# A planned instruction order: attention slots take only the time that stream stages leave

## The chip, the cores and the metric

The kernel runs on one NeuronCore of one Trainium2 chip. The metric is device time in microseconds (us) of one execution. The kernel before takes 3509.27 us, the median of three runs (3504.03 to 3510.40).

## The reference, cut to what matters

Four transformer layers in a row, in float32, on x of 4 batches x 1024 rows x 256 features. What bears on the change is the first layer (L0) and the last two (L2 and L3, which the kernel runs as one region):

```python
# L0: masked self-attention with 16 heads of 16, then cross-attention, then MLP
x = x + g_msa * (attn(q, k, v, mask) @ attn_out_W)
x = x + g_x * (attn(qc, kc, vc) @ co_W)              # 77 keys
x = x + g_mlp * (gelu(ln(x) @ mlp_W1 + mlp_b1) @ mlp_W2 + mlp_b2)
# L1: layernorm, 3 experts with a router, a gate; no attention over the rows
# L2: as L0 with full self-attention over 1024 keys, cross-attention, MLP
# L3: a further cross-attention over the 77 keys
x = x_q + (softmax(q k^T / 4) v) @ Wp + bp
```

In L0 the mask of this case leaves 256 of the 1024 keys alive, and the kernel finds that at run time and takes the short branch (`FEWR`). L2 works on all 1024 keys.

## The kernel before, in words

The work of a region (`FEWR` for L0; `L2R` for L2 and L3 together) is written as a list of tokens, `R.order`. All five engines walk the same list, each issuing its own part of every token, so the list is the program order on every engine. Each engine's queue is in order; a wait holds all that stands behind it.

There are two kinds of work:

- **Slots.** A slot is one step of self-attention for one key tile of 128 keys, 4 heads and 512 query rows: 4 score products (K=32 rows of the array each), ScalarE's 4 exponentials (line 1895), the 4 products with V of the slot before, and the "fills", score products `lead` slots ahead of which VectorE takes the row maximum (line 1564 in L2, 1561 in L0). L2 has 256 slots, 64 for each batch; L0 has 64, 16 for each batch. Some slots end with transposes: "nm" (line 1066) and "tail" (line 1055).
- **Stages of the streams.** Four streams prepare a batch (`p_tokens`: layernorm, V, Q and K). Eight streams (`o_tokens`: 4 batches x 2 halves of 512 rows) carry a half from its attention output to its end: output projection `oT`/`oP`, layernorm `lnA`/`lnB`/`lnT`, cross-attention, MLP `m1`/`m2`; in region L2 a second cross-attention (L3's) follows. Cross-attention is a chain: queries `cq`, maximum steps `cm` (4 per sequence, four VectorE reductions each, line 1717), `cn` (line 1180), exponentials `cs` (line 1943), products `cp`, transposes `ct` (line 1202). A stream of batch b opens when b's slots are over, so it runs beside the slots of batch b+1; the last batch's streams have no slots beside them. There are 12 cross-attention sequences beside slots in region L2 (3 batches x 2 halves x 2) and 6 in L0.

All matmuls of stages and slots take their PSUM bank from one ring of seven, in list order, and TensorE waits until the bank's last reader has freed it.

`overlapped(R)` (from line 525) is a planner that runs while the program is built. It keeps a clock `now`, gives every token a TensorE cost (`cost`: 3.2 us for a full slot of L2, 0.8 for `cm`, 6.9 for `m2`) and every dependence a latency (`needs`), and at each step places either the stage that has been ready longest or the next slot. A stage may be placed when it is ready and TensorE is free. What decides between a ready stage and a ready slot is a credit: each slot adds `R.share` (3.4 us in L2, 12.0 in L0, and never holds more), each stage takes its cost away, and with a credit of zero or less a ready slot goes first:

```python
state["credit"] = min(state["credit"] + R.share, R.share)     # place(), a slot
...
state["credit"] -= cost(R, tok)                                # place(), a stage
```

With a share of 3.4 the list of L2 has about one slot for every 3.4 us of stages as long as stages are ready. Going through the planner of the kernel before with its own costs, a slot is placed ahead of a ready stage 120 times among the 268 slot tokens of region L2, and 10 times among the 70 of L0. The order of layer 1 (`l1_order`) is written out by hand and has no planner.

Of the kernel before, what the change touches and what calls it, by code (L numbers as in the profile page):

```python
# [62 lines left out]
def pixart_kernel(nc, io):  # L63
    ctx = ExitStack()
    with ctx:
# [408 lines left out]
        def cost(R, tok):  # L474

            kind = tok[0]
            if kind == "slot":
                return (2.15 if tok[1] is not None else 0.0) + (1.05 if tok[2] is not None else 0.0) + 0.45 * len(tok[4]) + 0.45 * len(tok[5])
            if kind == "qk":
                return (3.4 if R.rope else 1.7) * (0.5 if tok[3] and R.few else 1.0)  # L480
            if kind == "v":
                return 1.7 if R.few else 3.5
            return {"lnT": 0.9, "oT": 0.9, "oP": 1.7, "cq": 1.7, "cm": 0.8, "cn": 0.5, "cs": 1.1, "cp": 1.1, "ct": 0.5, "m1": 3.4, "m2": 6.9}.get(kind, 0.0)
# [40 lines left out]
        def overlapped(R):  # L524
# [7 lines left out]
            state = {"now": 0.0, "t": -R.lead, "probs": 0, "turn": 0, "exp": 0.0, "credit": 0.0}  # L532
# [10 lines left out]
            def open_to(tok):  # L543

                t, kind = state["t"], tok[0]
                if kind in ("lnA", "lnB") and tok[1] == 0 and tok[2]:
                    b = tok[2]
                    if not all(k in ended for k in p_tokens(R, b - 1)):
                        return False
                if kind in ("lnB", "ct") and row_buffer(tok)[1]:  # L550
                    return rows[tok[-1]] is None
                if kind == "qk" and tok[1]:
                    return t >= (R.index(tok[1] - 1, 2 * tok[2] + 1, 1 if tok[3] else tok[4]) + 1) * R.per
                if kind == "v" and tok[1]:
                    if R.few:
                        return t > (tok[1] - 1) * R.total
                    return t > (R.index(tok[1] - 1, 2 * tok[2] + 1, 1) + 1) * R.per
                if kind == "oT" and tok[1] == 0:
                    return ("tail", R.index(tok[2], NG - 1, tok[3])) in ended and (tok[2] == 0 or all(k in ended for k in o_tokens(R, tok[2] - 1, tok[3])))
                if kind == "cs":  # L560
                    return state["probs"] == 0
                if kind == "cp":
                    return state["turn"] == 0
                return True

            def ready(tok):
                times = []
                for other, us in needs(R, tok):
                    if other not in ended:
                        return None  # L570
                    times.append(ended[other] + us)
                return max(times, default=0.0)

            def slot_ready():
                t, times = state["t"], [state["exp"]]
                fill = t + R.lead
                b, g, qh = R.block(fill // R.per)
                if fill < NB * R.total and fill % R.per == 0 and qh == 0 and g % 2 == 0:
                    for k in R.qk_steps(b, g // 2):
                        if k not in ended:  # L580
                            return None
                        times.append(ended[k] + (4.5 if R.rope else 2.0))
                if 1 <= t <= NB * R.total and (t - 1) % R.per == 0:
                    b, g, qh = R.block((t - 1) // R.per)
                    if ("v", b, 0 if R.few else g // 2) not in ended:
                        return None
                tok = slot_token(R, 0, NB * R.total, t)
                for q in tok[4]:
                    b, g, qh = R.block(q)
                    if b and ("oT", 0, b - 1, qh) not in ended:  # L590
                        return None
                return max(times)

            def place(tok):
                order.append(tok)
                kind = tok[0]
                state["now"] += cost(R, tok)
                ended[tok] = state["now"]
                if kind == "slot":
                    state["t"] += 1  # L600
                    state["credit"] = min(state["credit"] + R.share, R.share)
                    if tok[1] is not None:
                        state["exp"] = state["now"] + 1.1
                    for q in tok[4]:
                        ended["tail", q] = state["now"]
                elif kind in ("cs", "cp", "ct"):
                    state["probs"] += {"cs": 1, "cp": -1, "ct": 0}[kind]
                    state["turn"] += {"cs": 0, "cp": 1, "ct": -1}[kind]
                half, claim = row_buffer(tok)
                if half is not None:  # L610
                    rows[half] = tok if claim else None
                if kind != "slot" and state["t"] > 0:
                    state["credit"] -= cost(R, tok)
                for item in list(loads):
                    if item in loads and item[2] == 0.0 and all(k in ended for k in item[1]):
                        loads.remove(item)
                        place(item[0])

            def hidden_follows(tok):


                prior = next((k for k in reversed(order) if cost(R, k)), None)
                if tok[0] == "m1":
                    return tok[4] == 1 and prior == tok[:4] + (0,)
                return tok[0] == "cq" and R.l == 2 and tok[3] == 1 and prior == tok[:3] + (0,) + tok[4:]
# [5 lines left out]
            while state["t"] < end or any(h < len(s) for h, s in zip(heads, streams)):  # L631
                now = state["now"]
                for item in list(loads):
                    if item in loads and all(k in ended for k in item[1]) and max(ended[k] for k in item[1]) + item[2] <= now:
                        loads.remove(item)
                        place(item[0])
                found = []
                for n, s in enumerate(streams):
                    if heads[n] < len(s) and open_to(s[heads[n]]):
                        tok = s[heads[n]]  # L640
                        when = ready(tok)
                        if when is not None:
                            found.append((when, n, tok))
                free = [f for f in found if cost(R, f[2]) == 0.0 and f[0] <= now]
                if free:
                    when, n, tok = free[0]
                    heads[n] += 1
                    place(tok)
                    continue
                slot = slot_ready() if state["t"] < end else None  # L650
                work = sorted([f for f in found if f[0] <= now and cost(R, f[2])], key=lambda f: (not hidden_follows(f[2]), f[1] >= NB, f[0]))
                if work and (hidden_follows(work[0][2]) or slot is None or slot > now or state["credit"] > 0.0 or state["t"] <= 0):
                    when, n, tok = work[0]
                    heads[n] += 1
                    place(tok)
                elif slot is not None and (slot <= now or not work):
                    later = min([f[0] for f in found], default=slot)
                    if slot <= now or slot <= later:
                        state["now"] = max(now, slot)
                        place(slot_token(R, 0, NB * R.total, state["t"]))  # L660
                    else:
                        state["now"] = later
                else:
                    waits = [f[0] for f in found] + [max(ended[k] for k in item[1]) + item[2] for item in loads if all(k in ended for k in item[1])]
                    assert waits, (R.name, state, [s[h] for h, s in zip(heads, streams) if h < len(s)], loads)
                    state["now"] = min(waits) if min(waits) > now else now + 0.1
# [1486 lines left out]
```

## Time and profile before

| | us |
|---|---|
| median of three runs | 3509.27 |
| the profiled execution, its own time | 3505.52 |
| its span in the trace | 3503.7 |
| TensorE (PE) busy | 3300.4, 94% |
| VectorE (DVE) busy | 1840.0, 53% |
| ScalarE (ACT) busy | 1436.5, 41% |
| mean granted TensorE clock | 0.96 of full speed |

The span and what lies around it (1.8 us) make the profiled execution's own time. In the trace, preparation runs to about 100 us, region L0 to about 1000, layer 1 to about 1640, and region L2 from there to the end at 3503.7. The slots of region L2 lie between about 1700 and 3240 (its "nm" transposes, line 1066, run from 1700.4 to 3235); the streams of its first three batches start at about 1998. The rows on which the next section rests are below.

### The profile page before, as it was taken

The page shows a single profiled execution, that of the slowest core. Times are in us where ns is not written, and L with a number is a line of the kernel's source. Part 1 is how long each engine was busy: PE and PEld are TensorE (multiplying, and loading weights), DVE is VectorE, ACT ScalarE, POOL GpSimd, SP SyncE. Part 2 cuts the span into 40 slices and gives each one's busy share as a digit, 9 for nine tenths or more (in the row PEclk, how much of TensorE's full clock was granted, in tenths as well). Part 3 has the DMA queues.
Part 4 walks back from the last instruction along what each step waited for, and adds up shares of the span by engine and source line. Part 5 has one row for each costly group of instructions (what it writes and reads, how often), then busy time and mean ns, then how long its engine had stood idle before and what let it go on. Part 6 is the DMA issues. An engine that isn't in the chain of part 4 may idle for free.

```text
span 3503.7 us, 49090 instructions
## 1 busy us (share of the span) xinstructions
PE 3300.4 (94%) x19540; PEld 1823.4 (52%) x19540; DVE 1840.0 (53%) x3843; ACT 1436.5 (41%) x2607; POOL 244.6 (7%) x214
## 2 busy tenths in 40 slices
PE   6899999999889999998999999999999999999887
PEld 3555666657575666666433344534455344543364
DVE  4776544562412232324766775567755676556423
ACT  0344444344312222221355455554554645555333
POOL 1100100100100000001000010010100001010010
PEclk9999999989889999999899999999999999999898
DMA  5200000002000000001000000000000000000000
GB/s 166 90 6 1 8 20 4 25 1 95 16 22 1 0 1 0 1 1 55 1 1 1 1 7 4 1 25 7 7 4 16 10 7 7 4 16 16 1 1 13
DMA packets 57256, 57.99 MB, mean 17 GB/s; under 512 B 17728, under 2 KB 51248, under 8 KB 56764
## 3 DMA queue, kind: packets, MB, share of 16 engines
q1 hardware_dynamic: 57028, 54.79, 5.0%
q8 instruction: 163, 2.67, 0.3%
q14 instruction: 65, 0.53, 0.0%
HBM read 46.89 MB, written 7.89 MB: 16 GB/s over the span
## 4 chain that ended last, share of the span: by engine, by line
PE 89%; DVE 7%; ACT 2%; issue 1%; POOL 0%; DMA 0%; DVEq 0%; SPq 0%; ACTq 0%
PE ps L901 82%; PE ps L1075 3%; PE ps L1202 1%; DVE row_max_cross L1717 1%; PE ps L1055 1%; DVE max_halves L1564 1%; PE ps L1066 1%; ACT probs L1943 1%; DVE bn_stats L1618 1%; DVE xn_tok L1631 1%; DVE big L1723 1%; PE ps L1180 0%; ACT big L1895 0%; DVE bn_stats L1595 0%; DVE mean_var L1624 0%
## 5 line engine op out<-in xcount | busy, mean ns | idle before, releaser
L1895 ACT ACTIVATE big<-ps 128x512 f32<-128x512 f32 x1280 | 687.9, 598 | 795.1 <-PE ps L901 794.0
L901 PE MATMUL ps<-big 32*128 32x512 f32 (+2 forms) x5760 | 949.2, 603 | 15.9 <-DVE row_max L1561 4.3
L1564 DVE TENSOR_REDUCE max_halves<-ps 128x1 f32<-128x512 f32 x1024 | 653.0, 685 | 359.8 <-PE ps L901 359.0
L901 PEld LDWEIGHTS ps<-big 32*128 32x128 f32 (+1 forms) x5760 | 394.0, 188 | 497.5 <-issue 387.2
L901 PE MATMUL ps<-big,probs 128*32 128x512 f32 (+1 forms) x2688 | 378.7, 605 | 9.9 <-ACT big L1895 4.1
L901 PE MATMUL ps<-weights_mlp,big 128*128 128x256 f32 (+1 forms) x1248 | 334.7, 420 | 2.5 <-ACT big L1955 2.5
L901 PEld LDWEIGHTS ps<-weights_mlp,big 128*128 128x128 f32 x1248 | 235.4, 191 | 85.3 <-issue 57.0
L1601 DVE TENSOR_TENSOR x_tok<-ps,x_tok 128x512 f32<-128x512 f32 x112 | 77.4, 692 | 308.3 <-PE ps L901 308.3
L901 PE MATMUL ps<-x_T,weights_mlp 128*128 128x256 f32 x1024 | 229.6, 383 | 4.3 <-ACT x_T L1912 3.3
L1561 DVE TENSOR_REDUCE row_max<-ps 128x2 f32<-128x512 f32 x256 | 165.1, 686 | 128.0 <-PE ps L901 127.8
L1943 ACT ACTIVATE probs<-ps 77x512 f32<-77x512 f32 x384 | 196.4, 593 | 83.7 <-PE ps L901 83.7
L901 PEld LDWEIGHTS ps<-x_T,weights_mlp 128*128 128x128 f32 x1024 | 194.4, 191 | 37.4 <-issue 6.1
L901 PEld LDWEIGHTS ps<-big,probs 128*32 128x32 f32 (+1 forms) x2688 | 75.5, 113 | 236.7 <-issue 147.6
L2090 POOL TENSOR_SCALAR eps_tile<-mean_var 128x4 f32<-128x4 f32 x56 | 13.4, 240 | 2550.0 <-DVE mean_var L1624 2550.0
L1955 ACT ACTIVATE big<-ps,mlp_b 128x256 f32<-128x256 f32 x256 | 107.6, 471 | 180.4 <-PE ps L901 180.2
L1717 DVE TENSOR_REDUCE row_max_cross<-ps 128x4 f32<-128x308 f32 x384 | 155.1, 473 | 37.4 <-PE ps L901 36.6
L901 PE MATMUL ps<-big,k_v_cross 32*77 32x512 f32 (+1 forms) x832 | 155.8, 642 | 7.6 <-DVE big L1723 7.6
L901 PE MATMUL ps<-weights,x_T 128*128 128x256 f32 x640 | 159.2, 402 | 2.6 <-ACT x_T L1870 2.5
L901 PEld LDWEIGHTS ps<-weights,x_T 128*128 128x128 f32 x640 | 125.0, 201 | 43.9 <-issue 22.8
L901 PE MATMUL ps<-weights,big 128*128 128x256 f32 x640 | 145.5, 380 | 0.0
L1832 DVE SCALAR_TENSOR_TENSOR probs<-ps,o_T,probs 128x256 f32<-128x256 f32 x96 | 46.4, 484 | 178.2 <-PE ps L901 178.2
L2005 ACT ACTIVATE big<-ps,o_T 128x512 f32<-128x512 f32 x96 | 66.1, 688 | 177.5 <-PE ps L901 177.5
(223 smaller groups left out, 3387.9 us busy)
## 6 DMA issues: line engine op xcount, KB each, us to landing
weights_mlp<-in_L_xcond_mlp_W SPq DMA_DIRECT2D x5, 1024.0 KB, 5.3
weights_mlp<-in_L_xcond_W_mlp SPq DMA_DIRECT2D x5, 1024.0 KB, 5.4
x_tok<-in_x SPq DMA_DIRECT2D x4, 1024.0 KB, 9.4
out_y<-x_tok SPq DMA_DIRECT2D x8, 512.0 KB, 2.9
big<-in_L_xcond_e_w SPq DMA_DIRECT2D x3, 1024.0 KB, 9.8
gates_biases<-mod_rows SPq DMA_DIRECT2D x20, 128.0 KB, 5.2
big<-in_L_xcond_adaLN_W SPq DMA_DIRECT2D x1, 2304.0 KB
kc_groups<-x_tok SPq DMA_DIRECT2D x3, 616.0 KB, 7.4
```

The costliest lines, as they stand in the source:

```text
L901: return pe.matmul(out, lhsT, rhs, start=first, stop=last)
L1055: last = pe.transpose(PS[:, bank, i * P:(i + 1) * P], OT[:, c:c + P], ident[:, :])
L1075: last = pe.transpose(PS[:, banks[ft], (t % 4) * P:(t % 4 + 1) * P], rows[:, t, ft * P:(ft + 1) * P], ident[:, :])
L1561: dve.tensor_reduce(NM[:, 2 * qh + e, c:c + 2], PS[:, bank, :].rearrange("p (t n) -> p t n", t=2), AX.X, ALU.max, negate=True).then_inc(R. ...
L1564: dve.tensor_reduce(NMP[:, e, j, qt, hf:hf + 1], PS[:, bank, :], AX.X, ALU.max, negate=True).then_inc(R.frees(key), 1)
L1601: dve.tensor_tensor(x, PS[:, R.bank(key), :], x, ALU.add).then_inc(R.frees(key), 1)
L1717: dve.tensor_reduce(dst, src, AX.X, ALU.max, negate=True).then_inc(R.frees(key), 1)
L1832: dve.scalar_tensor_tensor(ROU[hf][:, t, :], PS[:, M.EXPERT[o % 2], 0:D], RP[:, 4 * hf + t, e:e + 1], ROU[hf][:, t, :], ALU.mult, ALU.add) ...
L1895: act.activation(PB[:, score % 2, j, :], PS[:, R.bank(key), :], ACT.Exp, scale=SCALE).then_inc(R.frees(key), 1)
L1943: act.activation(PC[0:NC, j, :], PS[0:NC, R.bank(key), :], ACT.Exp, scale=SCALE).then_inc(R.frees(key), 1)
L1955: last = act.activation(HT[hf][:, m, :], PS[:, R.bank(key), i % 2 * D:(i % 2 + 1) * D], ACT.Gelu_apprx_tanh, bias=B1[:, 0 if R.l == 0 else ...
L2005: act.activation(dst, PS[:, M.HIDDEN[q % 3], :], ACT.Silu, bias=ANC[:, m, b:b + 1]).then_inc(e_hsb, 1)
```

## The change

In `overlapped`, a ready stage no longer needs a credit. Whenever a stage is ready and TensorE is free in the plan, it is placed; a slot is placed when no stage is ready. The credit is still counted and has no effect. Costs, latencies, conditions for opening, and the engines' code for each token stay as they are, so every instruction is issued as often as before; only the order of tokens in regions L0 and L2 can differ. Layer 1 and the preparation don't change.

```diff
                 slot = slot_ready() if state["t"] < end else None
                 work = sorted([f for f in found if f[0] <= now and cost(R, f[2])], key=lambda f: (not hidden_follows(f[2]), f[1] >= NB, f[0]))
-                if work and (hidden_follows(work[0][2]) or slot is None or slot > now or state["credit"] > 0.0 or state["t"] <= 0):
+                if work and (hidden_follows(work[0][2]) or slot is None or slot > now or True):
                     when, n, tok = work[0]
```

## Rows read from the trace of the kernel before

**Rows 1.** The page: busy time of each engine, and its 40 slices.

```profile
PE 3300.4 (94%) x19540; PEld 1823.4 (52%) x19540; DVE 1840.0 (53%) x3843; ACT 1436.5 (41%) x2607; POOL 244.6 (7%) x214
...
PEclk9999999989889999999899999999999999999898
```

**Rows 2.** Stretches of region L2: us, engines' busy us, PEclk, DMA, GB/s.

```profile
1707.00:1990.00 283.00, 281.88 (x1764) 99.11 (x1764) 189.38 (x323) 148.57 (x280) 3.62 (x3) 1.00 0.00 1
1998.00:3240.00 1242.00, 1207.42 (x7948) 562.90 (x7944) 782.60 (x1532) 653.08 (x1192) 101.52 (x74) 0.99 0.03 9
3240.00:3504.00 264.00, 217.44 (x1228) 128.68 (x1227) 94.89 (x228) 92.56 (x172) 21.75 (x18) 0.86 0.01 5
```

**Rows 3.** Timeline of TensorE, slots alone: start us, us, what, count.

```profile
1745.07 2.93 PE L901 MATMUL ps<-big 32*128 32x512 f32 x16
1747.93 1.06 PE L901 MATMUL ps<-big,probs 128*32 128x512 f32 x8
1748.93 2.93 PE L901 MATMUL ps<-big 32*128 32x512 f32 x16
```

**Rows 4.** Groups by form, 1998 to 3240: busy, mean ns | idle before.

```profile
L1564 DVE TENSOR_REDUCE max_halves<-ps 128x1 f32<-128x512 f32 x716 | 459.7, 685 | 279.8 <-PE ps L901 279.0
L1895 ACT ACTIVATE big<-ps 128x512 f32<-128x512 f32 x723 | 390.9, 597 | 445.1 <-PE ps L901 444.7
...
L1717 DVE TENSOR_REDUCE row_max_cross<-ps 128x4 f32<-128x308 f32 x192 | 77.3, 474 | 10.7 <-PE ps L901 10.6
```

**Rows 5.** TensorE's waits, 1998 to 3240: total us, times, longest.

```profile
PE ps L901 <- ACT big L1895: 11.2, 16, 1.2
PE ps L901 <- DVE row_max_cross L1717: 9.0, 15, 0.7
```

**Rows 6.** Stretches with a fallen clock, and others, of 1998 to 3240.

```profile
1998.00:2028.00 30.00, 25.47 (x184) 14.06 (x180) 25.63 (x67) 9.54 (x18) 2.91 (x6) 0.83 0.06 14
...
2870.00:2900.00 30.00, 27.23 (x204) 13.32 (x200) 23.86 (x52) 12.09 (x23) 1.92 (x3) 0.94 0.07 19
2900.00:2950.00 50.00, 47.69 (x337) 18.39 (x334) 33.01 (x63) 27.59 (x52) 8.15 (x4) 0.93 0.00 1
...
3150.00:3180.00 30.00, 28.17 (x217) 13.69 (x210) 22.29 (x44) 13.99 (x27) 0.00 (x0) 0.94 0.00 1
```

**Rows 7.** Stretches of region L0, cross-attention and other stages in turn.

```profile
265.00:340.00 75.00, 69.75 (x649) 40.14 (x644) 52.49 (x103) 34.49 (x63) 0.00 (x0) 0.91 0.01 1
340.00:470.00 130.00, 129.18 (x776) 89.99 (x772) 65.32 (x149) 62.23 (x109) 12.25 (x13) 1.00 0.02 6
470.00:545.00 75.00, 68.76 (x556) 41.70 (x553) 44.50 (x90) 23.43 (x43) 7.78 (x5) 0.84 0.09 24
545.00:690.00 145.00, 144.53 (x889) 100.80 (x888) 70.19 (x143) 69.72 (x124) 9.74 (x9) 1.00 0.05 14
690.00:745.00 55.00, 48.76 (x429) 28.57 (x427) 32.45 (x71) 17.25 (x31) 7.65 (x5) 0.78 0.03 8
```

**Rows 8.** Exponentials of slots, 470 to 545, then 2080 to 2360.

```profile
L1895 ACT ACTIVATE big<-ps 128x512 f32<-128x512 f32 x16 | 8.7, 597 | 26.4 <-PE ps L901 26.4
...
L1895 ACT ACTIVATE big<-ps 128x512 f32<-128x512 f32 x157 | 84.9, 597 | 95.5 <-PE ps L901 95.4
```

**Rows 9.** Timeline of TensorE: three maximum steps in a row, then two.

```profile
2877.72 0.81 PE L901 MATMUL ps<-k_v_cross,x_T 32*128 32x154 f32 x16 [0.76 <-ACT big L1895]
2879.14 0.81 PE L901 MATMUL ps<-k_v_cross,x_T 32*128 32x154 f32 x16 [0.61 <-DVE row_max_cross L1717]
2880.68 1.41 PE L901 MATMUL ps<-k_v_cross,x_T 32*128 32x154 f32 x16 [0.74 <-DVE row_max_cross L1717]
...
2626.13 0.81 PE L901 MATMUL ps<-k_v_cross,x_T 32*128 32x154 f32 x16 [0.76 <-ACT big L1895]
2627.55 0.81 PE L901 MATMUL ps<-k_v_cross,x_T 32*128 32x154 f32 x16 [0.61 <-DVE row_max_cross L1717]
```

**Rows 10.** A stretch of region L0 at the fallen clock.

```profile
525.00:539.00 14.00, 13.19 (x119) 7.70 (x116) 7.61 (x19) 2.65 (x5) 0.00 (x0) 0.52 0.00 1
```

## The prediction

> **What bounds the kernel now.** I read the page first: TensorE is busy 94% of the span, VectorE 53%, ScalarE 41%, and the granted clock is nine tenths or more in all but a few slices [rows 1]. The chain of waits says the same; nearly all of it is TensorE's matmuls. A new order changes no instruction, so it can move the time only through what TensorE loses between and around its work: idle time, and time at the lower of its two clock levels (1.2 in place of 2.4 GHz). The second thing to read is therefore a table of stretches, and from it these two losses.
>
> In region L2 the slots alone (1707 to 1990) leave 1.1 us idle of 283 at clock 1.00. The stretch where stages of batches 0 to 2 run beside slots (1998 to 3240) leaves 1242 - 1207.4 = 34.6 us idle, at a clock of 0.99. The last batch's streams, which have no slots beside them (3240 to 3504), leave 46.6 idle of 264 at 0.86 [rows 2]. A slot alone takes TensorE 1748.93 - 1745.07 = 3.86 us [rows 3]; VectorE's four maxima take 4 x 0.685 = 2.7 and ScalarE's four exponentials 4 x 0.597 = 2.4 of it [rows 4]. So slots without stages are bound by TensorE too, and to push them into a bunch costs nothing.
>
> The idle time of the middle stretch is cross-attention's. TensorE waited in small pieces, 11.2 us in 16 waits named after the slots' exponentials and 9.0 in 15 named after `row_max_cross` [rows 5]. The first lot stands mostly at the head of a group of maximum steps as well: the timeline shows the steps in a row waiting 0.76, 0.61 and 0.74 us, since one step's sixteen matmuls take 0.8 us and its four reductions 4 x 0.474 = 1.9 [rows 4, 9]. The ring of seven banks fills, and TensorE goes at VectorE's pace.
>
> The clock's loss (stretch x (1 - clock)) is 30 x 0.17 = 5.1, 30 x 0.06 = 1.8, 50 x 0.07 = 3.5 and 30 x 0.06 = 1.8 us, 12.2 in all [rows 6]. Three of the four places are ones where three maximum steps stand in a row: there are five such places in this stretch, and the clock fell right behind three of them. The row at 2880.68 shows one: the third step's matmuls take 1.41 us in place of 0.81 [rows 9]. Where a slot parts the steps into two and one (seven places) it fell once.
>
> **The change part by part.** Every instruction stays, so the sum is a sum of differences in those two losses.
>
> *Layer 1, preparation, the last batch's streams.* Unchanged, 0. At the end there are no slots for a ready stage to compete with.
>
> *Region L2, where the order changes.* The credit held a ready stage back 120 times. Without it, the two half-streams of a batch run as fast as their chains let them, slots fill only what both leave open, and the rest of the 64 slots follows in a bunch. ScalarE's exponentials show what the mix is now: 157 in 280 us of L2, which is 39 slots, 10.5 per 75 us; region L0, whose credit of 12 us held back only 10 stages and which thus already follows nearly the rule of the change, has 16 in 75 us, 4 slots [rows 8]. So L0's cross-attention is the nearest sample of L2 after the change.
>
> What L0 loses there: 75 - 69.75 = 5.25, 75 - 68.76 = 6.24 and 55 - 48.76 = 6.24 us idle, 17.7 for six sequences, 3.0 each; and by the clock 75 x 0.09 = 6.8, 75 x 0.16 = 12.0 and 55 x 0.22 = 12.1, 30.9, or 5.1 each [rows 7]. L2 now has 12 sequences with 34.6 / 12 = 2.9 idle and 12.2 / 12 = 1.0 of clock. The idle per sequence is thus the same under both rules, and only the clock differs. The reason I see: in the plan, `cm` 0 to 2 become ready together, and without a credit nothing parts them. In L0 all six sequences have three in a row, and the clock fell behind each.
>
> Idle: seven more of twelve sequences get a third wait of 0.6 to 0.7 in a row; some already have it at another place. I take +3 us (bounds 0 and 12 x 0.74 = 9).
>
> Clock, low: the five rows of three in L2 lose 5.1 + 1.8 + 1.8 + 0 + 0 = 8.7 us, 1.7 each; twelve give 21, so 21 - 12 = +9. High: L0's 5.1 each gives 62 - 12 = +50. L0's slots are sparser and its chains shorter, but its fill rule is the one that L2 gets. I take the middle, +29. The far end is the last batch's streams with no slots at all: 264 x 0.14 = 37 us for four sequences, 9.2 each, which would give +99; slots still fill there, so I don't use it, except that the range leans up.
>
> *Region L0.* Ten slots move behind a stage. Six sequences already pay the dense price, and its other stages do well with few slots (0.8 us and 0.5 us idle in 130 and 145, clock 1.00 [rows 7]). I take 0, with 10 us either way: one fallen clock more or less per batch.
>
> *Queues.* SP's loads and GpSimd's gates stand in the same list. Stages come earlier, so a weight is asked for earlier, once its last reader has ended; the next reader, a batch later, has more time than now. Behind a bunch of slots no load waits for more than the bunch. 0.
>
> *What covers the stages now and is gone.* A stage placed at its planned readiness has no slack. The plan's latencies (2.7 us from `cs` to `cp`) stand beside 4 x 0.597 = 2.4 of ScalarE [rows 4]; in L0 they held, since its idle is that of the maximum steps. 0, and up to 5 us if a slot's exponentials stand in front.
>
> Sum: 3505.5 (the profiled execution's own time) + 3 + 29 = 3537.5. The median of the runs before is 3.8 us above that execution, so the median after should be 3541, slower by 0.9%.
>
> One rule of the Trainium skill speaks against the clock term. Its page "TensorE: Matmul & The Clock Gate", section "HAM oscillation — how this bites in real kernels", puts a fall of the clock down to one long gap between matmuls, such as a wait for a transfer. By that rule the largest waits here (0.76 us) could not bring one, the clock term is 0, and the sum is 3508.5. This trace disagrees: from 525 to 539 TensorE was busy 13.19 of 14 us with the clock at 0.52 [rows 10], and the waits ahead of it were 0.6 to 0.8 us each. The next section of that page, on cycling through PSUM banks, does describe falls from many small waits; by it the term stays.
>
> **The rivals.**
> (A) *The clock holds.* The falls might depend on what else stands around the steps; two of five rows of three in L2 passed without one, and stages rich in large matmuls run at 1.00 [rows 7]. Then only idle is left: +3, 3512. This is also about where the skill's rule would put it.
> (B) *Faster: the halves cover one another.* With no slots in between, the second half's cross-attention may fall beside the first half's MLP, whose `m2` takes 6.9 us in the plan and lies ready for any wait. If that parts the maximum steps in at least half of the sequences, and the banks are read out meanwhile, half of both losses goes: (34.6 + 12.2) / 2 = 23, so 3486. It decides if fewer than six of twelve sequences have three steps in a row. Against it: the steps of one half are ready at the same moment and the planner takes the longest ready first, and L0 has MLP beside cross-attention and has three in a row six times of six.
> (C) *Much slower: the bunches are emptier than L0's.* The streams meet with hardly a slot between, and lose as the last batch does, half of the way to +99: +52 on the clock and +9 idle, 3570.
> (D) *It does not do what it says:* slots are seldom ready in time when a stage is, and the order hardly moves: 3509. Against it: 120 stages held back.
>
> **How the numbers follow.** Forecast 0.50 (its own range 3518 to 3562), A 0.14, B 0.19, C 0.12, D 0.05. A measurement of this kernel can tell about 0.2%, 7 us. B gives nearly all of faster; D, most of A, and the forecast's low edge give the same; the rest is slower. That makes 0.20 faster, 0.15 the same, 0.65 slower. The range from 3496 to 3575 leaves out the lower part of B and the upper part of C, some 2 in 10.
>
> **What would show it.** In the new trace, cross-attention beside slots should have three maximum steps in a row in ten or more of twelve sequences, clocks of 0.8 to 0.95 in those stretches, and a loss by the clock between 1998 and 3240 of some 40 us in place of 12; idle time there within 5 us of 34.6; each of batches 1 to 3 ending in a run of 30 or more slots alone at 3.86 us; region L0 within 10 us of its length, and the stretch of the last batch and layer 1 unchanged. The forecast is wrong if the clock's loss in region L2 stays under 20 us, or if TensorE's idle time moves by more than 10. A wait for exponentials ahead of `cp` as a new large row would make the slack the cause in place of the clock.

## The result, and the profile after

The changed kernel takes 3546.88 us (median of four runs, 3540.15 to 3548.97) against 3509.84 for the kernel before on the same chip: the ratio, estimated from all the runs, is 1.0098, 95% interval 1.0077 to 1.0118. The forecast was 3541, so the sum came out; the terms of it did not.

The page after, its line of busy times and its granted clock, answers to [rows 1]: TensorE is busy 31.8 us longer (3332.2 against 3300.4) and the clock is the same.

```profile
span 3538.3 us, 49090 instructions
...
PE 3332.2 (94%) x19540; PEld 1847.1 (52%) x19540; DVE 1839.8 (52%) x3843; ACT 1429.9 (40%) x2607; POOL 245.2 (7%) x214
...
PEclk9999999999889999998999899999999999999988
```

The next two tables cut both traces at the same tokens: end of preparation, start of layer 1, the first "nm" transpose of region L2, then batches 0, 1, 2 and 3 of its slots, and what follows the last "nm". Columns as in [rows 2]. The kernel before:

```profile
100.00:1042.00 942.00, 885.71 (x5976) 587.30 (x5976) 495.94 (x1058) 380.28 (x686) 81.22 (x72) 0.94 0.08 24
1042.00:1700.00 658.00, 631.71 (x2328) 406.23 (x2328) 213.62 (x514) 151.00 (x263) 24.59 (x25) 0.97 0.02 8
1700.00:1966.00 266.00, 263.78 (x1645) 90.79 (x1646) 180.50 (x311) 138.17 (x263) 2.13 (x3) 1.00 0.00 1
1966.00:2408.00 442.00, 428.84 (x2808) 200.55 (x2808) 281.11 (x552) 230.64 (x419) 37.35 (x28) 0.99 0.03 9
2408.00:2844.00 436.00, 424.57 (x2800) 196.32 (x2792) 279.49 (x549) 228.98 (x417) 33.96 (x27) 1.00 0.03 9
2844.00:3235.00 391.00, 382.27 (x2509) 178.63 (x2506) 242.33 (x467) 207.12 (x379) 31.70 (x21) 0.98 0.03 10
3235.00:3504.00 269.00, 221.20 (x1252) 129.87 (x1252) 95.64 (x229) 96.03 (x178) 21.75 (x18) 0.86 0.01 5
```

The changed kernel:

```profile
100.00:1029.00 929.00, 877.30 (x5977) 583.14 (x5978) 497.94 (x1059) 379.64 (x686) 82.06 (x72) 0.94 0.08 25
1029.00:1687.00 658.00, 631.68 (x2329) 407.08 (x2329) 213.50 (x515) 150.74 (x263) 24.55 (x25) 0.97 0.03 8
1687.00:1954.00 267.00, 265.15 (x1648) 91.99 (x1649) 180.32 (x310) 138.27 (x263) 2.42 (x3) 1.00 0.00 1
1954.00:2415.00 461.00, 444.45 (x2812) 209.14 (x2811) 281.26 (x552) 228.91 (x420) 37.06 (x28) 0.97 0.03 8
2415.00:2876.00 461.00, 446.92 (x2790) 209.00 (x2788) 278.90 (x549) 226.96 (x417) 34.10 (x27) 0.97 0.03 8
2876.00:3279.00 403.00, 391.19 (x2508) 185.29 (x2504) 241.10 (x466) 205.57 (x378) 31.43 (x21) 0.99 0.03 9
3279.00:3538.00 259.00, 212.90 (x1254) 127.54 (x1252) 95.60 (x229) 95.69 (x178) 21.70 (x18) 0.89 0.01 5
```

Region L0 is 13 us shorter, layer 1 is the same, batches 1, 2 and 3 of L2 are 19, 25 and 12 longer, the end 10 shorter. In batch 1 TensorE is busy 15.6 us longer with the same instructions.

For each stretch I took three parts: gaps between TensorE's matmul records; half of the time that the clock's records show at 1.2 GHz; and the rest, time in which TensorE counts as busy at full clock. In us, from the profiled executions (the clock's part runs to the end of the span, some 2 us past the last matmul, so a difference of 1 or 2 us between two kernels in the last column says nothing):

| | idle | clock | rest |
|---|---|---|---|
| L0, before / after | 55.9 / 51.0 | 60.5 / 51.9 | 825.2 / 825.3 |
| layer 1 | 26.3 / 26.3 | 19.8 / 19.8 | 612.0 / 612.0 |
| L2 from its first "nm" | 78.6 / 86.7 | 49.7 / 56.7 | 1670.8 / 1703.8 |

The rest should not move when only the order does, and in L0 and layer 1 it doesn't. In L2 it grew by 33.0 us. It is not work. Here are two slots in the trace of the kernel before, each between two stages (columns: start us, us, what, matmul records). In the first, 8 records of scores and fills take 1.14 us, the products 1.07, 8 more 1.14, and it is 3.13 us from the slot's start to the next stage's.

```profile
2240.59 1.14 PE L901 MATMUL ps<-big 32*128 32x512 f32 x8
2241.66 1.07 PE L901 MATMUL ps<-big,probs 128*32 128x512 f32 x8
2242.65 1.14 PE L901 MATMUL ps<-big 32*128 32x512 f32 x8
2243.72 1.98 PE L901 MATMUL ps<-probs,weights 128*128 128x512 f32 x4
...
2257.61 1.14 PE L901 MATMUL ps<-big 32*128 32x512 f32 x8
2258.68 1.07 PE L901 MATMUL ps<-big,probs 128*32 128x512 f32 x8
2259.67 2.20 PE L901 MATMUL ps<-big 32*128 32x512 f32 x8
2261.80 0.64 PE L901 MATMUL ps<-probs,k_v_cross 77*32 77x512 f32 x4
```

The second slot shows that a stage doesn't always cover. Its last 8 records take 2.20 us: ScalarE was still busy with the stage before it (an activation of the MLP, then a table load of 1.28 us), the slot's exponential came late, and the last two weight loads waited 0.77 us for it.

Where a slot follows a slot, the 16 records between two groups of products take 2.93 us [rows 3], not 2 x 1.14 = 2.28. In the changed kernel the same, with the weight loads (PEld) and the readers beside it:

```profile
2738.09 2.93 PE L901 MATMUL ps<-big 32*128 32x512 f32 x16
2738.63 0.21 PEld L901 LDWEIGHTS ps<-big 32*128 32x128 f32 x3 [0.22 <-issue]
2739.06 0.21 PEld L901 LDWEIGHTS ps<-big 32*128 32x128 f32 x3 [0.22 <-issue]
2739.25 2.06 ACT L1895 ACTIVATE big<-ps 128x512 f32<-128x512 f32 x4 [1.54 <-PE ps L901]
...
2739.90 0.29 PEld L901 LDWEIGHTS ps<-big 32*128 32x128 f32 x2 [0.64 <-ACT big L1895]
```

Six of the second eight loads come in time; the last two wait 0.64 us for an exponential of the group just before. The view shows no idle time all the same, because the durations that it gives to matmuls are modelled and overlap that wait. A slot takes eight banks from a ring of seven, four for each group of steps: the fourth step of a group takes the bank of the first step of the group before it, whose reader needs 0.6 us. In the middle of a slot the products (1.07 us) stand in that place and cover it; at the end of a slot a stage covers it, and another slot doesn't. The planner's order has 78 slots directly behind a slot in L2 before and 172 after.

Counted over batches 1 to 3, from one start to the next, 16 records between two groups of products take 2.90 us in the mean, 77 times in the changed kernel and 9 times before. Two groups of 8 with a stage beside them take 1.32 and 1.23 before, 2.55 together: half of these groups take 1.07 or less, and some wait as the second slot above does. The difference of the means is 0.35 us, which is also 33.0 / 94.

The waits of the weight loads, for batches 1 and 2 of the kernel before (1966 to 2844), then of the changed one (1954 to 2876):

```profile
PEld ps L901 <- DVE max_halves L1564: 29.9, 37, 4.1
PEld ps L901 <- ACT big L1895: 22.2, 43, 0.8
```

```profile
PEld ps L901 <- DVE max_halves L1564: 69.2, 92, 1.5
PEld ps L901 <- ACT big L1895: 47.4, 88, 0.8
```

The second line holds the waits of those last two loads, among others. Of its waits, 21 stand ahead of loads for scores and fills before, and 75 after, where the plan has 11 and 73 slots directly behind a slot in these two batches. The first line is not a new wait: most of it stands ahead of the loads for the products, about 0.78 us each time, and the kernel before has the same gap there nearly as often, mostly under another name.

### The profile page after: what moved, and what is told of

Its sections match the earlier page's. It is cut to its first block, busy times and chain, and to the rows that moved or that the text cites. A ratio compares the mean times of both kernels' runs of the same rounds, so it can differ in the third digit from the quotient of the medians.

```text
span 3538.3 us, 49090 instructions
## 1 busy us (share of the span) xinstructions
PE 3332.2 (94%) x19540; PEld 1847.1 (52%) x19540; DVE 1839.8 (52%) x3843; ACT 1429.9 (40%) x2607; POOL 245.2 (7%) x214
## 4 chain that ended last, share of the span: by engine, by line
PE 89%; DVE 8%; ACT 1%; issue 1%; POOL 0%; DMA 0%; DVEq 0%; SPq 0%; ACTq 0%
PE ps L901 82%; PE ps L1075 3%; PE ps L1202 1%; DVE row_max_cross L1717 1%; PE ps L1055 1%; PE ps L1066 1%; DVE max_halves L1564 1%; DVE big L1723 1%; ACT probs L1943 1%; DVE bn_stats L1618 1%; DVE big L1589 1%; DVE bn_stats L1595 0%; PE ps L1180 0%; DVE xn_tok L1631 0%; DVE x_tok L1601 0%
## 5 line engine op out<-in xcount | busy, mean ns | idle before, releaser
L901 PE MATMUL ps<-big 32*128 32x512 f32 (+2 forms) x5760 | 975.9, 598 | 20.9 <-DVE big L1723 7.6
L901 PEld LDWEIGHTS ps<-big 32*128 32x128 f32 (+1 forms) x5760 | 410.9, 189 | 519.5 <-issue 370.6
```

The source lines that it names most:

```text
L901: return pe.matmul(out, lhsT, rhs, start=first, stop=last)
```

## The experiments

Two theories. A, the prediction's: slots in a bunch cost nothing; what L2 loses is the clock, which falls behind three maximum steps in a row. B: a slot directly behind a slot costs 0.3 to 0.35 us more (33.0 / 94 = 0.35), and idle and clock are the smaller part.

**The regions apart.** `l0_only` and `l2_only`:

```diff
-... or state["credit"] > 0.0 or state["t"] <= 0):
+... or R.l == 0 or state["credit"] > 0.0 or state["t"] <= 0):      # l0_only
+... or R.l == 2 or state["credit"] > 0.0 or state["t"] <= 0):      # l2_only
```

> The change in region L0 alone; L2 keeps its credit of 3.4. The two profiled executions put L0 at -13.4 us and L2 at +48. Theory 1 (the regions' effects add): 3510 - 13 = 3497, faster by 0.4%. Theory 2 (L0's gain is luck of one execution's clock): 3506 to 3512.

> The change in region L2 alone. Theory 1: 3510 + 48 = 3558, slower than the changed kernel by 12 us. Theory 2: 3547, as the changed kernel.

Measured: L0 alone 3494.94 against 3510.88, ratio 0.9961 (0.9937 to 0.9986); L2 alone 3557.66, 1.0128 (1.0071 to 1.0184). The effects add: -16 + 47 = +31 against +37. The change is two changes of opposite sign. In L0 the rest stays (824.3). Eight traces of these studies have L0's new order, with 50.3 to 52.6 us idle and 49.1 to 64.9 (mean 54.2) lost by the clock; four have the old one, with 54.0 to 56.3 and 60.5 to 66.1 (mean 63.4); the two `pv_late` kernels are left aside. So of the 13 to 16 us, about 4 are idle time and about 9 the clock.

**No three maximum steps in a row**, all else as changed:

```diff
+                if kind == "cm" and tok[3] == 2 and R.l == 2 and t < end:
+                    return state["slot"] > ended.get(("cm",) + tok[1:3] + (1,) + tok[4:], 0.0)
...
+                    state["slot"] = state["now"]                      # place(), a slot
```

> The changed kernel, but in region L2 the third maximum step of a sequence isn't placed until a slot has stood behind the second, so no three steps are in a row beside slots; slots placed directly behind a slot stay many (163 in place of 172; 78 before the change). Theory A, my prediction (the loss is the clock falling behind three steps in a row): all of L2's +48 or at least the 30 forecast go, 3500 to 3517. Theory B (a slot directly behind a slot costs about 0.3 us more than one behind a stage, 94 more of them are 28 us, and the clock is the rest): the clock's share of 7 to 15 us and 9 x 0.3 = 3 go, 3529 to 3537.

Measured: 3557.57, 1.0144 (1.0089 to 1.0199); its profiled execution has 3539.73, the changed kernel's 3540.15. Nothing was gained (the medians, from two chips, have overlapping intervals). The steps are parted, as its timeline shows (its line 904 is 901 of the kernel before): two, a slot, and the third behind it.

```profile
2421.55 0.81 PE L904 MATMUL ps<-k_v_cross,x_T 32*128 32x154 f32 x16 [0.49 <-ACT big L1898]
2422.97 0.81 PE L904 MATMUL ps<-k_v_cross,x_T 32*128 32x154 f32 x16 [0.61 <-DVE row_max_cross L1720]
2423.57 1.97 PE L904 MATMUL ps<-big 32*128 32x512 f32 x8
2425.47 1.07 PE L904 MATMUL ps<-big,probs 128*32 128x512 f32 x8
2426.47 1.14 PE L904 MATMUL ps<-big 32*128 32x512 f32 x8
```

Yet the clock is as low as in the changed kernel:

```profile
1956.00:2414.00 458.00, 442.58 (x2820) 208.40 (x2813) 282.18 (x554) 229.30 (x420) 37.92 (x28) 0.98 0.03 8
2414.00:2878.00 464.00, 447.53 (x2791) 209.87 (x2788) 281.29 (x548) 227.24 (x417) 33.80 (x27) 0.96 0.03 8
```

So three steps in a row are not needed for the clock to fall, and theory A falls. The falls do stand close behind maximum steps in every kernel, though. By the clock's records, in batches 1 to 3, the kernel before has four falls, three of them beginning 1.6 to 3.0 us behind the start of three steps in a row; the changed kernel has eight, seven of them 2.4 to 5.2 us behind such a start; and `cm_parted`, which has no three in a row, has eight too, five of them 2.6 to 4.4 us behind the start of two. What in dense cross-attention brings them isn't shown. L2's rest is 1701.4, as B says for 163 slots behind a slot. B's own number for this run (3529 to 3537) is missed too, since it had counted on the clock coming back.

**The other way: a smaller credit.** `even_28`, in L2 `self.share = 12.0 if few else 2.8`, and no credit in L0:

> The other way: no credit in L0, and in L2 a smaller credit of 2.8 us in place of 3.4, which spreads a batch's stages over all of its 64 slots. Slots directly behind a slot: 57 in place of 78; three steps in a row beside slots in 4 of 12 sequences in place of 5. Theory A: -13 for L0, 0 for L2, 3497. Theory B: -13 - 21 x 0.3 = -6, 3490. A third theory (later stages leave work over for the end): the cost of stages behind the last slot grows by 3.4 us in the plan, 3500.

Measured: 3490.51, 0.9935 (0.9909 to 0.9960). This is B's number, but not by B's term. L2's rest is 1672.9, no less than before: 6.8 and 7.9 us less in batches 1 and 2, as B says, and some 16 more in batch 3 and the end together. That TensorE is busy longer at the end, as the third theory says, is seen; why the saving is used up there isn't shown. What L2 gained, 12 us in the trace, is idle time (70.4 in place of 78.5) and clock. And against `l0_only` (3494.94, same chip) the smaller credit by itself is worth 4 us, which overlapping intervals don't settle.

**A larger credit.** `share_68`, 6.8 us in L2, L0 as before:

> The kernel before with L2's credit at 6.8 us in place of 3.4; L0 as before. 137 slots directly behind a slot in place of 78. Theory B: 59 x 0.3 to 0.35 = 18 to 21 us and a little of clock and idle, 3528 to 3536. If the loss is in starting stages without slack, a credit that still holds them back should cost little: 3510 to 3518.

Measured: 3542.20, 1.0093 (1.0064 to 1.0123), outside the expected range by 6 us. The rest is 1687.2: 16.4 us more for 59 more such slots, 0.28 each. Idle time is 91.4, 12.8 more than before, with the same single long waits for `row_max_cross` (4.8 us once, 1.8 or 1.9 three times) as in the changed kernel. So with a credit of twice the size L2 already loses 34 of the 47 us that it loses with none, and the slots' 0.28 us make only half of that; idle time is most of the other half.

**The cover moved.** `pv_late_before` and `pv_late_after`:

```diff
-                        if half == 0 and product is not None:
+                        if half == 1 and product is not None:
                             pv(product)
```

> The kernel before, with the four products with V moved from the middle of a slot to its end (both regions and every slot; all else in place). Theory B, in its detail: eight ring steps of a slot share seven banks, so the last of each group of four matmul steps waits for an exponential of the group just before it, unless something stands between the groups. In the kernel before the products stand in the middle and a stage stands at the end; only a slot directly behind a slot has nothing there (78 of 256 in L2). With the products at the end the middle is bare in every slot: the 178 others should pay about 0.3 us each, 53 us, 3563. If the extra cost of slots alone has another reason (weight loads, issue), the move changes nothing: 3510.

> The same move in the changed kernel. Theory B: 84 slots of L2 don't stand behind a slot and pay 0.3 us each, 25 us: 3572, so that the distance between the two orders shrinks from 37 us to about 9 (clock and idle time, less L0's gain). If the reason is another, the distance stays 37 us.

Measured: 3640.65, 1.0356 (1.0316 to 1.0396), and 3597.30, 1.0248 (1.0210 to 1.0286). The move costs more in the order with fewer slots in a bunch, as B says, but both times are above the expected 3563 and 3572, by 78 and 25 us. B had the distance between the orders shrink from 37 us to 9; it turned round. With the products at the slot's end, the order with more slots in a bunch is 43 us faster. In the traces 25 of the 43 us are in region L2 and 20 in L0. L2's rest grows by 87.4 us in the order before (178 slots not behind a slot, 0.49 each) and by 35.8 in the changed one (84, 0.43 each), against 0.3 expected. Region L0 is 40 and 33 us longer in these traces than in the same orders with the products in the middle, of which the expectations had nothing; why it is so much there wasn't tested. Slots alone hardly care: eight of them took 32.0 us and take 32.5. In the trace of `pv_late_before`, a slot between two stages now shows the wait of a slot alone, 2.99 us for its 16 records in place of 2 x 1.14:

```profile
2131.35 2.99 PE L901 MATMUL ps<-big 32*128 32x512 f32 x16
2134.27 1.07 PE L901 MATMUL ps<-big,probs 128*32 128x512 f32 x8
2135.27 3.72 PE L901 MATMUL ps<-weights,x_T 128*128 128x256 f32 x16
```

What decides is thus whether something stands between two groups of four steps on the ring. The rival on record, weight loads or issue, had both times as they were, 3510 and 37 us apart.

**The reader made shorter.** In region L2 each exponential of a slot covers 256 of its 512 columns; the other 256 are left out of the attention:

```diff
-   act.activation(PB[:, score % 2, j, :], PS[:, R.bank(key), :], ACT.Exp, scale=SCALE)
+   n = HALF // 2 if R.l == 2 else HALF
+   act.activation(PB[:, score % 2, j, 0:n], PS[:, R.bank(key), 0:n], ACT.Exp, scale=SCALE)
```

> The kernel before; in region L2 each exponential of a slot covers 256 of its 512 columns (the other half is left out). Theory B: what the last of four matmul steps waits for is an exponential of 0.6 us behind the group before it; cut to about 0.35 it leaves about 0.05 of the 0.3 us that a slot directly behind a slot costs, 78 x 0.25 = 20 us: 3490 or a little less. If the wait is on VectorE's maxima or on the array itself: 3510.

> The changed kernel with the same half of the exponentials left out. Theory B: 172 x 0.25 = 43 us off, 3504, so that the two orders stand 37 - 23 = 14 us apart. If the wait is on something else: the distance stays 37 us.

Measured: 3456.64, 0.9858 (0.9829 to 0.9886), and 3494.73, 0.9954 (0.9939 to 0.9969). Both are faster than expected by 33 and 9 us, and the medians stand 38 us apart, not 14. By the criterion on record (14 if B holds, 37 if not) these times speak for the rival. Only the parts in the traces speak for B. The rest of L2 is 1643.0 and 1657.8, 14.8 apart in place of 33.0, so the hidden wait did shrink by more than half; slots alone take 29.7 us for eight in place of 32.0. Idle time (70.6 and 83.2) and clock (34.5 and 48.1) stand 26 us apart, where they stood 15 apart. The clock's 7 of these 11 us are within what executions of one order differ by (49.7 and 42.9 for L2 before the change); the 4 us of idle time aren't explained. In the trace of `half_exp_after` the 16 records take 2.71 us (its line 1896 is the exponential):

```profile
1749.23 2.71 PE L901 MATMUL ps<-big 32*128 32x512 f32 x16
1750.83 0.29 PEld L901 LDWEIGHTS ps<-big 32*128 32x128 f32 x2 [0.42 <-ACT big L1896]
1751.88 1.07 PE L901 MATMUL ps<-big,probs 128*32 128x512 f32 x8
```

This is the closest test of the wait itself. The mean exponential went from 0.60 to 0.38 us, and the wait of the last two loads from 0.64 to 0.42, so it shrank by as much as its reader did. It isn't gone, and the 16 records don't take 2.28, because the group's first exponential starts 1.16 us after the group, as it did at full length (2739.25 behind 2738.09), and then still takes 0.38.

**Parting the steps where slots are spread.** `even_28_parted` (credit 2.8, none in L0, and the edit of `cm_parted`), `l0_parted` (credit 3.4), and the first again as `best_again`:

> The order with L2's credit of 2.8 and none in L0, and besides no three maximum steps in a row beside slots in L2 (before: 5 sequences, with 2.8: 4). A theory of idle time in the maximum steps: each third step waits 0.7 us, and parted they wait less; 4 to 10 us off, 3481 to 3487. From the run in which parting gave nothing: 3490, the same as with 2.8 alone.

> L2's credit at 3.4 as before, none in L0, and in L2 no three maximum steps in a row beside slots (5 sequences have them before). Parting gave nothing in the dense order and about 12 us with the credit of 2.8. If parting helps wherever slots are spread: 3497 less 5 to 10, 3487 to 3492. If it helps only together with the smaller credit: 3495.

> Credit 2.8 with parting once more, beside its neighbours on one chip: 3478 again, 30 us under the kernel before; if the first result had luck in its clock, 3485.

Measured: 3478.05, 0.9904 (0.9870 to 0.9939); 3493.88, 0.9950 (0.9932 to 0.9968); 3483.76, 0.9926 (0.9902 to 0.9950). With the credit of 3.4 parting gives nothing over `l0_only` (3494.94). With 2.8 it is 7 to 12 us under `even_28`, which overlapping intervals don't settle; region L2 in the traces takes 1779.8 and 1782.0 us against 1786.8. Against `l0_parted` on the same chip, which differs from it in the credit alone, `best_again` is 10 us faster (their intervals against the kernel before overlap a little). This version beats both kernels, the one before by 27 to 30 us on the same chips (some 16 of them are region L0's), and the changed one by 63 to 69 across chips. Its batches 1 and 2 answer to those of the two tables above:

```profile
1957.00:2389.00 432.00, 421.17 (x2766) 192.60 (x2763) 278.74 (x545) 227.98 (x417) 37.69 (x28) 0.99 0.02 7
2389.00:2820.00 431.00, 418.69 (x2785) 194.53 (x2785) 278.83 (x545) 227.09 (x414) 33.20 (x26) 1.00 0.03 9
```

## Why the prediction was right, and where it was not

The direction and the size of the sum were right (+32 forecast, +37 measured), and the size was luck. Between the two profiled executions lie 34.6 us, and the tables split them into +33 of rest, +3 of idle time and -2 of clock over the whole kernel; the forecast had 0, +3 and +29. An error of 33 us in one direction met an overstated clock and a region L0 that was 13 us off in the other.

- *"To push them into a bunch costs nothing"*: this step failed. It cost 33 us, the largest term. I read it from TensorE's busy share of 281.88 in 283 us [rows 2] and took a busy engine for a bound one. My own row had half of the answer: 2.93 us for 16 matmul records [rows 3], while 8 of them beside a stage take 1.14. The Trainium skill says so in "Perfetto Trace Analysis", section "Identifying the Most-Contended Engine": the matmul row's busy share is not a good measure of how near TensorE is to its limit. This trace agrees, with 0.65 us hidden in a busy 2.93. The page's reason, that pipelined instructions look smaller in a trace, isn't the one here, where the records cover a wait.
- *Clock, +29 (bounds +9 and +50)*: between the "nm" of batch 1's first slots and the last one it is 11.9 us before and 27.2 after, +15; some 40 was forecast in place of the 27.2. With the end, where it went from 37.8 to 29.4 though the order there is the same, region L2 has +7. The two pairs of traces with one order each (49.7 and 42.9 before, 56.7 and 49.8 after) give +7 as well. The term was mis-sized by a factor of two to four. Three maximum steps in a row came in twelve of twelve sequences, as forecast, and the seven falls behind them cost 24 us, 2.0 for each of the twelve: near the 1.7 of the low bound, and far from the 5.1 of region L0, with which the middle was formed. The reason given isn't borne out either, since parting the steps brought nothing.
- *Idle, +3 (bounds 0 and +9)*: 33.3 to 42.4 us in batches 1 to 3, +9, the upper bound. TensorE's waits for `row_max_cross`, 9.0 us in 15 [rows 5], became 24.5 in 22, and the longest is 4.8 us, where the prediction reckoned with 0.6 to 0.76 for each (it calls 0.76 the largest wait, while [rows 5] has 1.2):

```profile
PE ps L901 <- DVE row_max_cross L1717: 24.5, 22, 4.8
PE ps L901 <- DVE big L1723: 6.4, 7, 3.6
PE ps L901 <- ACT probs L1943: 3.0, 4, 0.8
```

- *Region L0, 0 within 10*: -13 in the trace, -16 in the run of its own. Out of the bounds; L0 was no finished sample of the dense order, as it had something left to gain.
- *The prediction's signs of being wrong*: neither came about (27.2 us of clock in batches 1 to 3, where under 20 was the sign; idle time +9, where over 10 was), though the largest term was missing. None of them looked at the price of the slots.
- *Queues, layer 1*: 0, as said. *Slack*: no large row ahead of `cp` appeared (`ACT probs` 3.0 us), as said.
- Each of batches 1 to 3 does end in some 40 slots in a bunch, broken only by the next batch's Q and K, as forecast; the wrong part was their price.
- Rival B's condition (fewer than six of twelve sequences with three in a row) didn't come about; rival A, with no clock term, was nearer to the +7 of region L2 than the forecast was, and missed the bunches as well.

The planner itself had a price for it, three times too high: after a slot it lets the next one start 1.1 us later (`state["exp"]`), and its planned length of L2 went from 1698.1 to 1800.1, 102 us for 94 such slots, of which 33 were measured. The prediction doesn't use it.

Open: why the clock falls behind maximum steps, if three in a row aren't needed; why L0's clock gains; why idle time grows as it does without a credit and with one of 6.8 us; and why the hidden wait that the credit of 2.8 saves in batches 1 and 2 comes back at the end.

## What to carry to other kernels

A stage put between two equal steps is worth its own time plus the wait that it covers, so a filler should be spread over the gaps and not be used up at once. Here a credit of 3.4 us beat none by 47 us in region L2. A credit near stages / slots (about 2.8 us) with parted steps was 10 us under 3.4 with parted steps, with intervals that overlap a little; by itself its lead of 4 us isn't settled. Before calling a stretch bound by TensorE, compare the same matmuls' time in two surroundings; if eight records take 1.14 us in one place and sixteen 2.93 in another, the difference is a wait. A change that covers several regions should be predicted and timed region by region.

## What the runs showed that I had not expected

Where four products stand between groups of matmuls on a ring of seven banks decides almost 4% of this kernel: moving them by half a slot, with no instruction added, cost 133 us (1.0356), 97 of them in region L2 and 40 in L0 by the traces. And the time at the lower clock in a stretch with one and the same order differs between executions and chips by several us (49.1 to 64.9 us of loss in region L0's new order), so that a clock term of that size can't be read from one trace.
